# Attention scores and maxima as two 64-row tiles on a key stack without zero halves

## The chip, the cores and the metric

The kernel runs on one core of one Trainium2 chip. The metric is the device time of one execution in microseconds, lower is better. A core has TensorE (PE; its weight loads are listed apart as PEld), VectorE (DVE), ScalarE (ACT), GpSimd (POOL) and SyncE (SP), which here only issues DMAs. Each runs its own instructions in order and waits on semaphores.

## What is computed

16 batches of x, each 256 tokens by 256 features, with a condition vector of 64 numbers per batch. Four layers follow one another; all in fp32, with products of high and low parts where precision asks for it.

```
_L0: x = x + a_alpha * attention(gamma*rmsnorm(x)+beta)     # 16 heads of 16, softmax(scale*q.k)
     x = x + f_alpha * (silu(h @ gate.T) * (h @ hidden.T)) @ out.T + out_b
_L1: u = h @ up.T; val, gate = split(u); h = val * gelu(gate)
     y = quantised(h) @ ternary(down).T;  x = y + x
_L2: x = x + relu(x @ Wd_b.T + bd) @ Wu_b.T + bu            # Wd_b, Wu_b made from the condition
_L3: layer norm of x, plus tanh(condition @ lin_w.T + lin_b), scaled
```

The change touches the attention of _L0 alone: for each head the product of 256 queries and 256 keys over 16 features, its maximum over the keys, and exp(scale * (product - maximum)).

## The kernel before, in words

**The loop.** `whole` unrolls the first three and the last three runs and loops over the rest. A run works on several batches at once, each at another stage: `a` is in attention, `f` (one batch earlier) in the gated layer of _L0 and the up projection of _L1, `g` (two earlier) in the rest, `nxt` (one later) in its norm and its q, k, v projection. Every engine has its own `run` (lines 324, 411, 642, 906, 1228), written out by hand, and this order is what each engine executes. Loop periods are all alike.

**The stacks.** `project_qk` (458) puts q and k of the next batch into PSUM. ScalarE copies them as fp32r (`split_qk`, 777), VectorE subtracts (`low_qk`, 1030), so there is a high and a low part. SP writes both to HBM (`stack_qk`, 287, line 298) and reads them back as stacks (line 312), twelve loads of 128 KB: per head 16 rows of q high, q low, q high against k high, k high, k low, and row 48 for the maximum against a row of ones. Even heads lie on partitions 0 to 48, odd heads on 64 to 112. `q_stack` holds 8 pairs; `k_stack` holds 16 heads, each with the other parity's half zero (memset at line 438), so that one matmul over 128 rows gives the scores of one head. Row 48 of `q_stack` is set to zero by two small DMAs (303) while the maxima are computed, later it is filled with them (359).

**Maxima.** `max_scores(b, n)` (477) is one matmul of 512 columns: 128 queries of a pair against the 256 keys of both heads, into one of banks 0 to 2. `row_max` (1036) reduces a bank on VectorE. On TensorE's `run`, for c from 0 to 9: `gate(f, c)` (534), `max_scores(a, 2c)` and `(a, 2c+1)`, `ffn_out(f, c-2)` (550). Then `max_turn` (493) transposes the maxima, ScalarE copies them (`max_row_out`), SP puts them into row 48.

**Scores.** `scores(b, h)` (499) is two matmuls of 256 columns with the keys as weights, into bank 0 or 1; ScalarE's `exps` (798) takes a bank per head. Between them stand `mlp_down`, `norm_g`, `y_turn`, `adapter_down`, `adapter_up` of other batches and, after every four heads, `attend` (510), eight fp32 matmuls in four column tiles of 128x32, listed as 16 since each takes two passes.

**After it.** den_guess on ScalarE, `normalise` and `normalised`, `centre` and then `low_qk` of the next batch on VectorE; the write and the read of the stacks run while TensorE does `project`, `project_v` and `up` (566) and the first `gate`. `norm_a` (454, 1021) has its mean and its Newton steps in bank 4, `norm_g` (562, 1125) in bank 5.

Of the kernel before, what the change touches and what calls it, by code (L numbers as in the profile page):

```python
# [15 lines left out]
F32 = mybir.dt.float32  # L16
# [60 lines left out]
def build(nc, xT, condT, w_cond, w_qkvT, w_oT, w_ghT, w_outT, out_b, w_upT, w_downT,  # L77
          w_hyper, head_rows, adapt_w, adapt_b, bd, bu, ln_w, ln_b, lin_b, ident_in, out):
    with ExitStack() as ctx:
# [10 lines left out]


# [45 lines left out]
        k_stack = sb("k_stack", [P, H, T], F32R)  # L137
# [3 lines left out]
        zero_row = few_rows[32:32 + NPAIR, :]  # L141
# [71 lines left out]
        qk_dram_w, stack_dma = sem("qk_dram_w", 32), sem("stack_dma", 16 * 14)  # L213
# [9 lines left out]
        max_mm, max_red = sem("max_mm", 16), sem("max_red", 16)  # L223
        max_t, max_row = sem("max_t"), sem("max_row")
        s_mm, s_exp, pv_mm = sem("s_mm", 16), sem("s_exp", 16), sem("pv_mm", 4)
# [50 lines left out]
        with nc.Block() as block:  # L276

            @block.sync
            def _(sp):
# [7 lines left out]
                def stack_qk(b):  # L287
# [14 lines left out]
                    for a in range(2):  # L302
                        sp.dma_start(q_stack[64 * a + 48:64 * a + 49, :, :].bitcast(F32), zero_row).then_inc(stack_dma.sem, 16)
                    sp.wait_ge(qk_dram_w.sem, qk_dram_w.at(b))
                    for dram, dst, parts in ((q_dram, q_stack, (0, 1, 0)), (k_dram, k_stack, (0, 0, 1))):
                        for a in range(2):
                            for c, part in enumerate(parts):
                                src = dram[:, part].rearrange("(m a r) n -> a r m n", a=2, r=DH)[a]
                                at = 64 * a + DH * c
                                to = dst[at:at + DH, :, :] if dst is q_stack else \  # L310
                                    dst[at:at + DH].rearrange("r (m a) n -> r a m n", a=2)[:, a]
                                sp.dma_start(to.bitcast(F32), src).then_inc(stack_dma.sem, 16)  # L312
# [69 lines left out]
                sp.wait_ge(init_pool.sem, 2)  # L382
                sp.wait_ge(init_dve.sem, 4)
                for a in range(2):
                    sp.dma_start(k_stack[64 * a + 48:64 * a + 49].rearrange("r (m a) n -> r a m n", a=2)[:, a].bitcast(F32),
                                 one_row).then_inc(init_dma.sem, 16)
# [11 lines left out]
            def _(pool):  # L398
# [39 lines left out]
                pool.memset(k_stack[:].bitcast(F32), 0.0).then_inc(init_pool.sem, 1)  # L438
# [9 lines left out]
            def _(pe):  # L448
# [28 lines left out]
                def max_scores(b, n):  # L477
                    pair, qt = n // 2, n % 2
                    if n == 0:
                        pe.wait_ge(stack_dma.sem, stack_dma.at(b))  # L480

                    if n == 0:
                        pe.wait_ge(qk_lo.sem, qk_lo.at(b, 1))
                    if n == 1:
                        pe.wait_ge(qk_lo.sem, qk_lo.at(b, 2))
                    if n == 2:
                        pe.wait_ge(v_ready.sem, v_ready.at(b))
                    if n >= 3:
# [918 lines left out]
```

## Time and profile before

| | us |
|---|---|
| runs | 1147.42, 1151.02, 1153.07 |
| median | 1151.02 |
| profiled execution, its own span | 1152.7 |
| PE busy | 1006.3 |
| PEld busy | 848.4 |
| DVE busy | 791.2 |
| ACT busy | 534.8 |
| POOL busy | 197.4 |

The profile is one execution. PE busy adds up durations that contain the way through the array, and matmuls overlap; the distance between starts is what a matmul costs in a flow. An idle time stands in square brackets with what ended it. The last instruction that used the engine may still be listed as busy while the array stands empty, so a hole of 0.1 us between two matmuls shows in their starts alone. In the chain of waits a piece names the engine, the tile it wrote and the line; "SPq" is the issue of a DMA.

### The profile page before, as it was taken

The page shows a single profiled execution, that of the slowest core. Times are in us where ns is not written, and L with a number is a line of the kernel's source. Part 1 is how long each engine was busy: PE and PEld are TensorE (multiplying, and loading weights), DVE is VectorE, ACT ScalarE, POOL GpSimd, SP SyncE. Part 2 cuts the span into 40 slices and gives each one's busy share as a digit, 9 for nine tenths or more (in the row PEclk, how much of TensorE's full clock was granted, in tenths as well). Part 3 has the DMA queues.
Part 4 walks back from the last instruction along what each step waited for, and adds up shares of the span by engine and source line. Part 5 has one row for each costly group of instructions (what it writes and reads, how often), then busy time and mean ns, then how long its engine had stood idle before and what let it go on. Part 6 is the DMA issues. An engine that isn't in the chain of part 4 may idle for free.

```text
span 1152.7 us, 22223 instructions
## 1 busy us (share of the span) xinstructions
PE 1006.3 (87%) x7362; PEld 848.4 (74%) x7362; DVE 791.2 (69%) x1755; ACT 534.8 (46%) x1100; POOL 197.4 (17%) x235
## 2 busy tenths in 40 slices
PE   5159679999999999999999999999999999998964
PEld 4024659788887879697878878797969788886852
DVE  3445367777777777777777777877777777776552
ACT  2245264545545363645454453636364544535330
POOL 2341101111121211021111212120211112121210
PEclk9679799999999999999999999999999999999985
DMA  9998506060604224060707042241606070510000
GB/s 334 264 279 310 73 2 120 1 130 2 126 3 80 49 55 74 33 96 1 128 1 128 1 84 45 61 68 38 91 1 128 1 128 1 91 31 10 10 19 9
DMA packets 78049, 89.45 MB, mean 78 GB/s; under 512 B 18672, under 2 KB 64640, under 8 KB 75392
## 3 DMA queue, kind: packets, MB, share of 16 engines
q1 hardware_dynamic: 71792, 62.81, 28.9%
q0 software_dynamic: 2304, 16.78, 4.0%
q10 hardware_dynamic: 3920, 9.44, 2.2%
q8 instruction: 19, 0.31, 0.1%
q14 instruction: 14, 0.11, 0.0%
HBM read 63.14 MB, written 25.31 MB: 77 GB/s over the span
## 4 chain that ended last, share of the span: by engine, by line
PE 52%; DMA 17%; DVE 13%; SPq 7%; issue 5%; ACT 4%; POOL 1%; DVEq 0%; ACTq 0%; POOLq 0%
PE bank L545 14%; DMA k_stack<-k_dram 10%; PE bank L506 7%; PE bank L557 7%; PE bank L490 5%; SPq L312 5%; DMA k_dram<-probs 5%; PE bank L582 4%; PE bank L516 4%; PE bank L451 4%; DMA k_stack<-few_rows 1%; PE bank L620 1%; DVE probs L1033 1%; PE bank L593 1%; PE bank L614 1%
## 5 line engine op out<-in xcount | busy, mean ns | idle before, releaser
L1042 DVE TENSOR_REDUCE neg_max<-bank 128x2 f32<-128x512 f32 x256 | 165.2, 684 | 45.6 <-PE bank L490 45.6
L418 POOL TENSOR_TENSOR act_lo<-act_f,act_hi 128x256 fp32r<-128x256 f32 x128 | 94.4, 738 | 444.6 <-ACT act_hi L839 444.6
L804 ACT ACTIVATE probs<-bank 128x512 f32<-128x512 f32 x256 | 138.4, 592 | 37.0 <-PE bank L506 35.6
L833 ACT ACTIVATE silu_g<-bank 128x256 f32<-128x256 f32 x128 | 49.1, 384 | 219.3 <-PE bank L545 219.2
L490 PE MATMUL bank<-k_stack,q_stack 128*128 128x512 f32 x256 | 86.2, 419 | 45.2 <-DMA k_stack<-k_dram 44.3
L506 PE MATMUL bank<-q_stack,k_stack 128*128 128x256 f32 x512 | 108.3, 329 | 5.7 <-DMA q_stack<-few_rows 2.4
L506 PEld LDWEIGHTS bank<-q_stack,k_stack 128*128 128x128 f32 x512 | 76.6, 192 | 45.6 <-ACT probs L804 31.9
L582 PE MATMUL bank<-up_hi,h_hi 128*128 128x256 f32 x512 | 106.7, 289 | 1.3 <-DVE act_u L1145 0.6
L545 PE MATMUL bank<-h_hi,gh_hi 128*128 128x256 f32 x512 | 103.5, 284 | 3.6 <-DVE h_lo L1103 3.6
L545 PE MATMUL bank<-h_lo,gh_hi 128*128 128x256 f32 x512 | 103.5, 284 | 0.0
L545 PE MATMUL bank<-h_hi,gh_lo 128*128 128x256 f32 x512 | 102.9, 283 | 0.0
L582 PE MATMUL bank<-up_lo,h_hi 128*128 128x256 f32 x512 | 101.7, 280 | 0.0
L582 PE MATMUL bank<-up_hi,h_lo 128*128 128x256 f32 x512 | 101.7, 279 | 0.0
L868 ACT ACTIVATE gelu_g<-bank 128x256 f32<-128x256 f32 x128 | 49.1, 384 | 104.6 <-PE bank L582 104.0
L403 POOL TENSOR_TENSOR xc<-xc,y 128x512 f32<-128x512 f32 x16 | 20.7, 1294 | 435.5 <-DVE y L1015 435.5
L1109 DVE TENSOR_TENSOR act_f<-bank,silu_g 128x256 f32<-128x256 f32 x128 | 53.9, 421 | 56.6 <-ACT silu_g L833 55.6
L1145 DVE TENSOR_TENSOR act_u<-bank,gelu_g 128x256 f32<-128x256 f32 x128 | 54.0, 422 | 50.9 <-ACT gelu_g L868 50.9
L545 PEld LDWEIGHTS bank<-h_hi,gh_hi 128*128 128x128 f32 x512 | 81.3, 190 | 7.2 <-issue 4.5
L582 PEld LDWEIGHTS bank<-up_hi,h_hi 128*128 128x128 f32 x512 | 79.6, 189 | 5.6 <-DVE act_u L1145 4.1
L516 PE MATMUL bank<-probs,v_aug 128*32 128x256 f32 x1024 | 69.4, 389 | 14.1 <-ACT probs L804 14.1
L490 PEld LDWEIGHTS bank<-k_stack,q_stack 128*128 128x128 f32 x256 | 40.3, 193 | 53.6 <-DMA k_stack<-k_dram 35.2
L545 PEld LDWEIGHTS bank<-h_hi,gh_lo 128*128 128x128 f32 x512 | 79.5, 190 | 0.0
(150 smaller groups left out, 2193.4 us busy)
## 6 DMA issues: line engine op xcount, KB each, us to landing
hyper<-w_hyper POOLq DMA_DIRECT2D x16, 1024.0 KB, 8.2
q_stack<-q_dram SPq DMA_DIRECT2D x96, 128.0 KB
k_stack<-k_dram SPq DMA_DIRECT2D x96, 128.0 KB
q_dram<-probs SPq DMA_DIRECT2D x16, 512.0 KB, 2.8
k_dram<-probs SPq DMA_DIRECT2D x16, 512.0 KB, 3.6
delta_dram<-hyper_s ACTq DMA_DIRECT2D x16, 256.0 KB, 6.4
x_res<-xT SPq DMA_DIRECT2D x16, 256.0 KB, 7.9
out<-xc SPq DMA_DIRECT2D x16, 256.0 KB, 8.3
```

The lines of the kernel that those rows point to most:

```text
L312: sp.dma_start(to.bitcast(F32), src).then_inc(stack_dma.sem, 16)
L418: pool.tensor_tensor(act_lo[:, c % 3, :], act_f[:, c % 2, :], act_hi[:, c % 3, :].bitcast(F32), ALU.subtract).then_inc(g_lo.sem, 1)
L490: pe.matmul(bank[n % 3][:], q_stack[:, pair, qt * P:(qt + 1) * P], k_stack[:, 2 * pair:2 * pair + 2, :], start=True, stop=True).then_inc(m ...
L506: mm = pe.matmul(halves(h % 2)[:, k, :], k_stack[:, h, k * P:(k + 1) * P], q_stack[:, h // 2, :], start=True, stop=True)
L516: mm = pe.matmul(at[32 * j:32 * j + 32, t % 2, :], v_aug[:, k, 4 * t + j, :], probs[:, (4 * t + j) % SLOTS, k, :], start=(k == 0), stop=(k ...
L545: mm = pe.matmul(at[:, x, :], w[:, d, x * F + c * P:x * F + (c + 1) * P], h[:, d, :], start=(n == 0), stop=(n == 5))
L557: mm = pe.matmul(halves(3)[:, m, :], w[:, c, m * P:(m + 1) * P], h[:, c % 3, :], start=(c == 0 and m == 0 and n == 0), stop=(c == FC - 1 a ...
L582: mm = pe.matmul(at[:, x, :], h[:, d, t * P:(t + 1) * P], w[:, d, x * F + c * UW:x * F + (c + 1) * UW], start=(i == 0), stop=(i == 5))
L804: act.activation(probs[:, h % SLOTS], halves(h % 2), ACT.Exp, scale=float(H / D) ** 0.5).then_inc(s_exp.sem, 1)
L1042: dve.tensor_reduce(neg_max[:, qt, :, pair:pair + 1].rearrange("p a o -> p (a o)"), halves(n % 3), AX_X, ALU.max, negate=True).then_inc(ma ...
L1109: dve.tensor_tensor(act_f[:, c % 2, :], halves(4 + c % 2)[:, 1, :], silu_g[:, c % 2, :], ALU.mult)\
L1145: dve.tensor_tensor(act_u[:, t, c * UW:(c + 1) * UW], halves(7 - n % 2)[:, 0, :], gelu_g[:, n % 2, :], ALU.mult).then_inc(u_dve.sem, 1)
```

## The change

Scores and maxima are matmuls on 64-row tiles: `tile_position=(0, 0)` for the even heads, `(64, 0)` for the odd ones, over 48 or 49 rows, issued in turn. `k_stack` holds 8 pairs like `q_stack`, without zero halves; its memset, that of `q_stack`, the zero row and the two DMAs of line 303 are gone. `max_scores(b, d)` does two pairs for 128 queries in four matmuls of 256 columns, with one semaphore step, into two banks, one for each parity; `row_max` reduces one parity of two pairs. `scores(b, m)` does a pair of heads in four matmuls with one step; the heads rotate over banks 0, 1 and 4. So the mean and the Newton steps of `norm_a` move from bank 4 to bank 5, where `norm_g` has its own: `norm_g` waits for the third Newton step of `norm_a`, and `norm_a` stands behind `ffn_out(6)` and waits for the last `gated`. In TensorE's order `mlp_down(g, 1)` stands between the first and second pair of scores, and `norm_g` behind the second.

```diff
+        def score_bank(h):
+            return halves((0, 1, 4)[h % 3])
-        k_stack = sb("k_stack", [P, H, T], F32R)
+        k_stack = sb("k_stack", [P, NPAIR, T], F32R)
...
-                    for a in range(2):
-                        sp.dma_start(q_stack[64 * a + 48:64 * a + 49, :, :].bitcast(F32), zero_row).then_inc(stack_dma.sem, 16)
...
-                pool.memset(k_stack[:].bitcast(F32), 0.0).then_inc(init_pool.sem, 1)
...
-                    mean(bank[4][:, 0:T], h1).then_inc(n1_pe.sem, 1)
+                    mean(bank[5][:, 0:T], h1).then_inc(n1_pe.sem, 1)
...
-                def max_scores(b, n):
-                    pair, qt = n // 2, n % 2
...
-                    if n >= 3:
-                        pe.wait_ge(max_red.sem, max_red.at(b, n - 2))
-                    pe.matmul(bank[n % 3][:], q_stack[:, pair, qt * P:(qt + 1) * P],
-                              k_stack[:, 2 * pair:2 * pair + 2, :], start=True, stop=True).then_inc(max_mm.sem, 1)
+                def max_scores(b, d):
+                    m, qt = d // 2 * 2, d % 2
...
+                    if d >= 1:
+                        pe.wait_ge(max_red.sem, max_red.at(b, 2 * d - 1))
+                    for i in range(2):
+                        for a in range(2):
+                            r = slice(64 * a, 64 * a + 48)
+                            mm = pe.matmul(halves((2 * d + a) % 3)[:, i, :], q_stack[r, m + i, qt * P:(qt + 1) * P],
+                                           k_stack[r, m + i, :], start=True, stop=True, tile_position=(64 * a, 0))
+                    mm.then_inc(max_mm.sem, 1)
...
-                def scores(b, h):
...
-                    if h >= 2:
-                        pe.wait_ge(s_exp.sem, s_exp.at(b, h - 1))
+                def scores(b, m):
...
+                    if m >= 1:
+                        pe.wait_ge(s_exp.sem, s_exp.at(b, 2 * m - 1))
                     for k in range(TT):
-                        mm = pe.matmul(halves(h % 2)[:, k, :], k_stack[:, h, k * P:(k + 1) * P], q_stack[:, h // 2, :],
-                                       start=True, stop=True)
+                        for a in range(2):
+                            r = slice(64 * a, 64 * a + 49)
+                            mm = pe.matmul(score_bank(2 * m + a)[:, k, :], k_stack[r, m, k * P:(k + 1) * P], q_stack[r, m, :],
+                                           start=True, stop=True, tile_position=(64 * a, 0))
                     mm.then_inc(s_mm.sem, 1)
...
-                def norm_g(b):
+                def norm_g(b, nxt):
                     pe.wait_ge(n3_act.sem, n3_act.at(b, 1))
+                    if nxt:
+                        pe.wait_ge(n1_dve.sem, n1_dve.at(nxt, 3))
...
                         if a and c < FC:
-                            max_scores(a, 2 * c)
-                            max_scores(a, 2 * c + 1)
+                            max_scores(a, c)
...
                         if f and c >= 2:
                             ffn_out(f, c - 2)
+                        if nxt and c == FC:
+                            if starts(a):
+                                pe.wait_ge(ternary.sem, 2)
+                            if f:
+                                pe.wait_ge(g_dve.sem, g_dve.at(f))
+                            norm_a(nxt)
...
                     if a:
                         scores(a, 0)
+                    if g:
+                        mlp_down(g, 1)
+                    if a:
                         scores(a, 1)
-                    if g:
-                        mlp_down(g, 1)
                     if f:
-                        norm_g(f)
-                    if a:
-                        scores(a, 2)
-                        scores(a, 3)
+                        norm_g(f, nxt)
                     for t in range(4):
...
                             if t < 3:
-                                scores(a, 4 * t + 4)
-                                scores(a, 4 * t + 5)
+                                scores(a, 2 * t + 2)
...
                             attend(a, t)
                             if t < 3:
-                                scores(a, 4 * t + 6)
-                                scores(a, 4 * t + 7)
+                                scores(a, 2 * t + 3)
...
-                    pair, qt = n // 2, n % 2
-                    dve.wait_ge(max_mm.sem, max_mm.at(b, n + 1))
+                    d, a = n // 2, n % 2
+                    m, qt = d // 2 * 2, d % 2
+                    dve.wait_ge(max_mm.sem, max_mm.at(b, d + 1))
...
-                    dve.tensor_reduce(neg_max[:, qt, :, pair:pair + 1].rearrange("p a o -> p (a o)"), halves(n % 3), AX_X, ALU.max,
+                    dve.tensor_reduce(neg_max[:, qt, a, m:m + 2], halves(n % 3), AX_X, ALU.max,
                                       negate=True).then_inc(max_red.sem, 1)
```

## Rows read from the trace of the kernel before

**Rows 1.** Page, part 1, TensorE: busy time, share, instructions.

```profile
PE 1006.3 (87%) x7362; PEld 848.4 (74%) x7362; DVE 791.2 (69%) x1755; ACT 534.8 (46%) x1100; POOL 197.4 (17%) x235
```

**Rows 2.** Windows: stretch, length; busy us per engine (instructions), clock, DMA share, GB/s.

```profile
568.64:588.60 19.96, 19.17 (x153) 18.20 (x153) 16.22 (x33) 5.76 (x16) 5.29 (x8) 1.00 0.11 29
568.64:631.90 63.26, 59.63 (x450) 51.66 (x451) 47.66 (x108) 31.75 (x67) 10.20 (x13) 1.00 0.32 59
```

**Rows 3.** Chain of waits in one period: start us, us, what.

```profile
599.04 0.86 PE bank L614 x4
...
612.84 1.21 DVE probs L1033 x2
614.13 3.56 DMA k_dram<-probs
...
622.82 8.96 DMA k_stack<-k_dram
```

**Rows 4.** Timeline, PE: start, us, line, operation, count [idle before <- releaser].

```profile
568.64 0.72 PE L490 MATMUL bank<-k_stack,q_stack 128*128 128x512 f32 x2 [1.01 <-DMA k_stack<-k_dram]
...
588.60 0.39 PE L496 MATMUL bank<-ident,neg_max 128*16 128x128 f32 x2 [0.78 <-DVE neg_max L1042]
...
594.21 1.13 PE L451 MATMUL bank<-h,mean_w 128*128 128x256 f32 x4 [0.30 <-ACT h L757]
...
606.10 0.42 PE L516 MATMUL bank<-probs,v_aug 128*32 128x256 f32 x4 [0.94 <-ACT probs L804]
```

**Rows 5.** Timeline, PE, around the last maxima of the period.

```profile
586.25 0.40 PE L545 MATMUL bank<-h_lo,gh_hi 128*128 128x256 f32 x2
586.49 0.61 PE L490 MATMUL bank<-k_stack,q_stack 128*128 128x512 f32 x2
586.94 0.28 PE L557 MATMUL bank<-act_hi,fo_hi 128*128 128x256 f32 x1
```

**Rows 6.** Timelines, PE and PEld, short windows where scores and attend meet.

```profile
596.75 0.50 PE L506 MATMUL bank<-q_stack,k_stack 128*128 128x256 f32 x2
597.18 0.42 PE L516 MATMUL bank<-probs,v_aug 128*32 128x256 f32 x4
...
597.42 0.13 PEld L516 LDWEIGHTS bank<-probs,v_aug 128*32 128x32 f32 x4
...
597.64 0.61 PE L516 MATMUL bank<-probs,v_aug 128*32 128x256 f32 x8
598.18 0.19 PEld L506 LDWEIGHTS bank<-q_stack,k_stack 128*128 128x128 f32 x1 [0.41 <-ACT probs L804]
...
604.42 0.74 PE L506 MATMUL bank<-q_stack,k_stack 128*128 128x256 f32 x4
```

**Rows 7.** Groups by line and form, weight loads, 300 to 1000 us: busy, mean ns.

```profile
L506 PEld LDWEIGHTS bank<-q_stack,k_stack 128*128 128x128 f32 x352 | 51.8, 188 | 25.4 <-ACT probs L804 18.4 <-issue 4.1
...
L516 PEld LDWEIGHTS bank<-probs,v_aug 128*32 128x32 f32 x704 | 18.4, 109 | 24.6 <-ACT probs L804 12.6
```

**Rows 8.** Timeline of SP's DMA issues in the period.

```profile
614.55 2.02 SPq L303 DMA_DIRECT2D q_stack<-few_rows  x2
```

**Rows 9.** Timeline, ACT: exponentials 0 and 1, 2 and 3, 4 and 5, 14 and 15.

```profile
594.06 1.06 ACT L804 ACTIVATE probs<-bank 128x512 f32<-128x512 f32 x2
595.61 1.09 ACT L804 ACTIVATE probs<-bank 128x512 f32<-128x512 f32 x2 [0.48 <-PE bank L506]
...
597.41 1.07 ACT L804 ACTIVATE probs<-bank 128x512 f32<-128x512 f32 x2
...
604.96 1.08 ACT L804 ACTIVATE probs<-bank 128x512 f32<-128x512 f32 x2 [0.69 <-PE bank L506]
```

**Rows 10.** Timeline, DVE: third Newton step of norm_a.

```profile
595.76 0.42 DVE L1015 SCALAR_TENSOR_TENSOR y<-bank,y 128x256 f32<-128x256 f32 x1
```

**Rows 11.** The start: timeline of POOL, and the chain of waits.

```profile
2.03 3.53 POOL L438 MEMSET k_stack<- 128x4096 f32 x1
...
18.88 16.53 DMA k_stack<-few_rows
```

More of the change, by code:

```diff
@@ L212, in build @@
         x_in_dma, x_res_dma = sem("x_in_dma", 32), sem("x_res_dma", 32)
-        qk_dram_w, stack_dma = sem("qk_dram_w", 32), sem("stack_dma", 16 * 14)
+        qk_dram_w, stack_dma = sem("qk_dram_w", 32), sem("stack_dma", 16 * 12)
         max_dma = sem("max_dma", 32)
@@ L664, in run @@
                             max_turn(a)
-                        if nxt and c == FC:
-                            if f:
-                                pe.wait_ge(g_dve.sem, g_dve.at(f, 7))
-                            norm_a(nxt)
                         if f and c >= 2:
                             ffn_out(f, c - 2)
+                        if nxt and c == FC:
[4 more added lines that the diff above has]
+                            norm_a(nxt)
                         if starts(a) and c in (1, 3, 5, 7):
@@ L679, in run @@
                         scores(a, 0)
-                        scores(a, 1)
                     if g:
                         mlp_down(g, 1)
+                    if a:
+                        scores(a, 1)
                     if f:
-                        norm_g(f)
-                    if a:
-                        scores(a, 2)
-                        scores(a, 3)
+                        norm_g(f, nxt)
                     for t in range(4):
@@ L735, in _ @@
                     for c in range(DC):
-                        mm = pe.matmul(bank[5][:, (m * DC + c) * NB:(m * DC + c + 1) * NB],
+                        mm = pe.matmul(bank[4][:, (m * DC + c) * NB:(m * DC + c + 1) * NB],
                                        cond_w[:, m * D + c * P:m * D + (c + 1) * P], cond_t[0:C, 0:NB],
@@ L774, in guess_a @@
                         act.wait_ge(n1_dve.sem, n1_dve.at(b, back=1))
-                    guess(y1, 4, eps_rms, n1_act, b, 2)
+                    guess(y1, 5, eps_rms, n1_act, b, 2)
                 def split_qk(b):
@@ L798, in exps @@
                 def exps(b, h):
-                    act.wait_ge(s_mm.sem, s_mm.at(b, h + 1))
+                    act.wait_ge(s_mm.sem, s_mm.at(b, h // 2 + 1))
                     if h == 0:
@@ L803, in exps @@
                         act.wait_ge(pv_mm.sem, pv_mm.at(b, (h - SLOTS) // 4 + 1))
-                    act.activation(probs[:, h % SLOTS], halves(h % 2), ACT.Exp, scale=float(H / D) ** 0.5).then_inc(s_exp.sem, 1)
+                    act.activation(probs[:, h % SLOTS], score_bank(h), ACT.Exp, scale=float(H / D) ** 0.5).then_inc(s_exp.sem, 1)
                 def den_guess(b, u):
@@ L988, in _ @@
                 for c in range(DC):
-                    act.activation(tanh_t[:, c, :], bank[5][:, (14 + c) * NB:(15 + c) * NB], ACT.Tanh,
+                    act.activation(tanh_t[:, c, :], bank[4][:, (14 + c) * NB:(15 + c) * NB], ACT.Tanh,
                                    bias=lin_b_c[:, c:c + 1]).then_inc(tanh_act.sem, 1)
@@ L996, in _ @@
                 split_qk(Batch(0))
-                act.wait_ge(init_dve.sem, 4)
+                act.wait_ge(init_dve.sem, 2)
                 copy_v(Batch(0))
@@ L1293, in _ @@
                 dve.memset(eps_ln, EPS_LN).then_inc(consts.sem, 1)
-                dve.memset(q_stack[:].bitcast(F32), 0.0).then_inc(init_dve.sem, 1)
-                dve.memset(zero_row, 0.0).then_inc(init_dve.sem, 1)
                 dve.memset(one_row, 1.0).then_inc(init_dve.sem, 1)
@@ L1302, in _ @@
                 dve.wait_ge(cond_mm.sem, 1)
-                src = bank[5][:, 0:16 * NB].rearrange("p (m c b) -> p m c b", m=8, c=DC)
+                src = bank[4][:, 0:16 * NB].rearrange("p (m c b) -> p m c b", m=8, c=DC)
                 dve.wait_ge(tanh_act.sem, DC)
```

28 lines of the change are left out of this document (10 added, 18 removed).

## Prediction

> **What bounds the kernel now.** I read the page first: TensorE is busy 87% of the span [rows 1]. Then one loop period cut into stages, the chain of waits through it, and the timelines at the seams. A period lasts 63.26 us, from 568.64 to 631.90, at full clock [rows 2]. The chain through it has three kinds of stretch. In the first 18.8 us it goes from one TensorE group to the next: gate, maximum scores and ffn_out run without a gap. From 592.3 to 605.5 the scores (L506) alternate with the 16 exponentials on ScalarE; ScalarE stops for scores (0.48 us before exp 2, 0.69 before exp 14) [rows 9], TensorE for exponentials (0.94 us before the last attend) [rows 4]. Last comes a DMA stretch: low_qk, 3.56 us for the write of k, twelve issues, and 8.96 us until the stack is in SBUF [rows 3]. TensorE, busy with `up` meanwhile, waits only 1.0 us at its end [rows 4]. So a us of TensorE counts in full in the first stretch, partly in the second, and in the third only beyond that 1.0 us.
>
> **The prices.** (a) In steady flow matmuls of 256 columns start 0.12 us apart (two take 0.40, one alone 0.28) [rows 5]: the weight load of the next hides behind the one before. (b) Where the array's shape changes there is a hole. The second of two score matmuls starts at 596.75 + 0.50 - 0.28 = 596.97; the first of the 128x32 tiles starts at 597.18, 0.21 later instead of 0.12 [rows 6]. Going back, the last tile matmul starts at 597.64 + 0.61 - 0.38 = 597.87 and the next full load at 598.18, 0.31 later; a steady fp32 matmul takes 0.215 (four in L614's 0.86) [rows 3]. Either way about 0.10 us stand empty. (c) The load itself is then in the open: in the burst of four at 604.42 the last starts 0.74 - 0.28 = 0.46 after the first load, where three steady steps are 0.35 [rows 6]. A change of shape into 128-column weights thus costs 0.10 + 0.11 = 0.21 us.
> (d) Do two row tiles run at once? No row shows two of them. The nearest are the four column tiles of L516: four matmuls fit into 0.42 us of which one alone is 0.38 to 0.40, so they start within 0.03 us, and four of their loads fit into 0.13 [rows 6]. The other end is one after another. A load of 128 columns lasts 188 ns, one of 32 columns 109 [rows 7], so 128 columns hold the weight path some 128/96 x 79 = 105 ns, nearly a steady step. If the two tiles' loads had to queue, a pair would take 0.23 and nothing would be won. I take "at once", as the column tiles do.
> The Trainium skill (TensorE: Matmul & The Clock Gate, What overlaps and what doesn't) says that a load overlaps running matmuls only where its row group differs. That favours "at once"; but the loads of (a) hide behind matmuls on the same rows, so the trace does not bear out its "only".
>
> **Phase one, gate and maxima.** Removed per group: two matmuls of 512 columns, which push the next L557 from 586.49 to 586.94, 0.45 us [rows 5]. Added: four matmuls of 256 columns in two pairs between full-array work on both sides: 0.10 empty, 0.11 load, two steps of 0.115, 0.10 empty, 0.11 load, together 0.63 to 0.65. Difference +0.18. Seven of a batch's eight groups pay it; before the first TensorE stands idle for the DMA and pays nothing: 1.2 us. TensorE's 0.78 us of idle time before max_turn [rows 4] gives no cover: it waits for the last row_max, and row_max(14) now waits for the whole last group instead of half of it. VectorE has room, 16.2 of 19.96 us busy [rows 2]. **+1.2 us a batch**, 15 batches with a gate beside them: +18.
>
> **Phase two, scores and exponentials.** I stepped through it with the offsets of the rows: the second pair starts 0.22 after the group's first load (0.12 plus the open 0.11); ScalarE starts 0.32 after the last matmul's start (604.42 + 0.22, then exp 14 at 604.96); exponentials follow 0.49 apart (1.08 - 0.59); TensorE goes on 0.65 after the start of the exponential it waits for (605.45 to 606.10) [rows 4, 6, 9]. In the frame of the period shown:
> - Scores 0 wait for the maxima's DMA as before; mlp_down follows 0.1 earlier. Scores 1 now wait for exp 0 (594.06) and load at 594.71, so exp 2 starts at 595.26 instead of 595.61.
> - norm_g now waits for the third step of norm_a's Newton iteration, since both use bank 5. That step ended at 595.76 + 0.42 = 596.18 [rows 10], now at about 596.06. The mean starts at 596.12 instead of 594.21 [rows 4]. Queued behind it on TensorE are y_turn, scores 2 and attend 0; for its result wait guess_g and, behind that on ScalarE, exp 4. Exp 4 moves from 597.41 to 598.16: +0.75.
> - From there each group S of scores stands between other shapes, where it was so only next to attend. S3 loads at 599.06, S4 at 600.56, S5 at 602.00, S6 at 603.50, S7 at 604.93, each because TensorE arrives only then, not because a bank is late. Exp 6 starts at 599.60, exp 8 at 601.10, exp 12 at 604.04, exp 14 at 605.47 instead of 604.96.
> The two steps of 0.12 saved per pair of heads nearly pay for the changes of shape; the third bank for scores is rarely what is waited for. **Exp 15 ends 0.5 us later**, 16 batches: +8. All up to low_qk (den_guess, normalise, centre) hangs on it and shifts with it.
>
> **Phase three and the start.** The twelve stack loads keep size, count and order. The key stack is now contiguous in SBUF, but its source rows in HBM are cut as before: 0, and from the twelve issues and 8.96 us I see no reason for more than 0.5 either way. The two zero-row DMAs (2.02 us of SP's queue, until 616.57) [rows 8] lie within SP's wait for the write of k, which ends at 617.69 [rows 3]: their removal gains nothing. norm_a moves behind ffn_out(6), with its user guess_a still behind the table load: 0. At the start the memset of the old stack held GpSimd 3.53 us ahead of three weight loads; but the chain there runs over the ones row of the key stack, which took 16.53 us behind other loads of its queue [rows 11]: -1, within -3 and +3, since the three loads now enter a full DMA earlier.
> **Sum:** 1152.7 + 18 + 8 - 1 = 1178 on the profiled execution, whose span lies 1.7 above the median of 1151.0; on that median **1176**, with a range of its own of 1162 to 1192 (a change of shape between 0.17 and 0.25, norm_g's delay between 0.3 and 0.8).
>
> **Rivals.** *Row tiles change shape for nothing (faster).* Every row of (b) is of a column split. Then a group of maxima costs 0.23 instead of 0.45: 8 x -0.22 + 0.1 = -1.7 us, 15 times; in phase two norm_g's delay is made up and exp 15 comes 0.3 earlier, 16 times. With the start -31: 1120. It decides in phase one: below 0.11 a change, that phase gains. For it: the rows keep their weights and moving data apart without any new cut of the columns. Against: both ways, into the split and out of it, show the same 0.10.
> The Trainium skill (TensorEngine Tiling (Array Packing), Key Properties) says that a change of tiling mode, not just of tile, drains TensorE, and lists row and column splits as modes alike. By that rule this rival is out, and the L506 to L516 rows agree with it. The same page's Theoretical Speedup of up to 2x for a small dimension of 64 would, alone, give 1120.
> *Half the price.* At 0.1 a change phase one moves by 0 and phase two by 0.1 to 0.2: 1148 to 1155.
> *One after another (slower still).* A group takes 0.24 more: phase one +1.9 a batch, in phase two six groups in the chain, +1.4. +29 + 22: 1227. For it: loads of 128 columns fill the weight path, those of L516 are of 32. This is also the case in which the change doesn't do what it says.
>
> **Numbers.** Forecast 0.56, shape for nothing 0.20, half price 0.11, one after another 0.13. The range 1118 to 1194 takes in the first three and leaves out the last. 0.5% of 1151 is 5.8 us, about what a measurement of this kernel can tell from no change. Faster: the first rival and a little of the half price, 0.22. Same: 0.09. Slower: 0.69.
>
> **What would show it.** In the changed trace: the starts of the two tiles' matmuls (0.01 us apart, or 0.12); from the last gate matmul to the first load of the maxima 0.21, and again out of it; 0.64 added by a group, 0.23 or 0.87; from the stack's landing to max_turn 21.1 instead of 19.96; exp 4 0.75 and exp 15 0.5 later against square_g; TensorE's wait for the stack still near 1 us; a period near 65.0. I am wrong if changes of shape are free for rows, if VectorE's maxima set phase one instead of TensorE, if TensorE's 1.0 us behind the DMA turns into a longer or shorter wait, or if the start moves by more than 3 us.

## The result and the profile after

| | before | after |
|---|---|---|
| median, us | 1150.06 (1147.42 to 1153.07, 4 runs) | 1187.87 (1183.63 to 1189.88, 4 runs) |
| ratio, 95% interval | | 1.0333 [1.0303, 1.0362] |
| profiled execution, span | 1152.7 | 1185.2 |
| mean granted clock | 0.959 | 0.941 |

The changed kernel is slower by 37.8 us. The forecast was slower by 25.

Page of the changed kernel, part 1. It answers to [rows 1].

```profile
PE 1015.9 (86%) x7618; PEld 821.1 (69%) x7618; DVE 793.9 (67%) x1753; ACT 537.6 (45%) x1100; POOL 193.8 (16%) x234
```

TensorE did 256 matmuls more and was busy 10 us longer, the span grew by 32.5. So 23 us of the loss stand outside TensorE's busy time.

Windows of the changed kernel: from the landing of the stack to max_turn, and one whole period. The columns are those of [rows 2].

```profile
584.32:605.31 20.99, 20.23 (x168) 17.97 (x168) 16.43 (x33) 6.32 (x18) 5.21 (x8) 1.00 0.11 27
584.32:649.78 65.46, 59.36 (x468) 49.36 (x468) 48.40 (x108) 32.45 (x69) 10.18 (x13) 1.00 0.32 57
```

The first stretch takes 20.99 where [rows 2] have 19.96, with VectorE no busier.

PE's timeline of the changed kernel around a group of maxima, then its weight loads, then max_turn.

```profile
588.56 0.40 PE L545 MATMUL bank<-h_lo,gh_hi 128*128 128x256 f32 x2
588.89 0.50 PE L486 MATMUL bank<-k_stack,q_stack 48*128 48x256 f32 x4
589.32 0.38 PE L557 MATMUL bank<-act_hi,fo_hi 128*128 128x256 f32 x1
589.54 0.28 PE L557 MATMUL bank<-act_hi,fo_lo 128*128 128x256 f32 x1
...
588.89 0.30 PEld L486 LDWEIGHTS bank<-k_stack,q_stack 48*128 48x128 f32 x4
...
605.36 0.39 PE L493 MATMUL bank<-ident,neg_max 128*16 128x128 f32 x2 [0.81 <-DVE neg_max L1042]
```

Read it by starts, as [rows 5]. The last gate matmul starts at 588.56 + 0.40 - 0.28 = 588.68. The first load of the maxima comes 0.21 later and the first full load after them at 589.32. The four tile matmuls fill 0.50, so the second pair starts 0.22 after the first (0.12 plus 0.10 of open load); the records' own starts put the two tiles of a pair 0.004 and 0.002 us apart. From the last gate matmul to ffn_out it is 0.64; in [rows 5] it is 586.94 - 586.37 = 0.57, and there the next matmul follows after the steady 0.12, here after 0.22. That makes 0.17 a group here, where gate matmuls stand before it and ffn_out behind it.

PE's, ACT's and DVE's timelines of the changed kernel where norm_g now waits. They answer to [rows 4, 9, 10].

```profile
611.49 0.50 PE L506 MATMUL bank<-q_stack,k_stack 49*128 49x256 f32 x4 [0.93 <-ACT probs L803]
612.88 1.13 PE L446 MATMUL bank<-h,mean_w 128*128 128x256 f32 x4 [0.89 <-DVE y L1014]
...
610.85 2.26 ACT L803 ACTIVATE probs<-bank 128x512 f32<-128x512 f32 x4
614.04 0.48 ACT L760 ACTIVATE y<-bank,columns 128x256 f32<-128x256 f32 x1 [0.93 <-PE bank L446]
...
614.92 1.09 ACT L803 ACTIVATE probs<-bank 128x512 f32<-128x512 f32 x2
...
612.40 0.42 DVE L1014 SCALAR_TENSOR_TENSOR y<-bank,y 128x256 f32<-128x256 f32 x1
```

The third Newton step of norm_a ends at 612.82, norm_g's mean starts at 612.88, guess_g (L760) at 614.04 and exp 4 at 614.92: 4.07 us after exp 0, where before it is 597.41 - 594.06 = 3.35 [rows 9]. Scores 1, the only matmuls between 610.56 (the end of mlp_down) and 612.88, stand between two holes of about 0.9 us.

The same place 195 us earlier, in one of the three middle periods (of 13) in which something more happens. Timeline of PE, then windows; the granted clock is the number after the five engines:

```profile
416.16 0.50 PE L506 MATMUL bank<-q_stack,k_stack 49*128 49x256 f32 x4 [0.94 <-ACT probs L803]
417.54 2.07 PE L446 MATMUL bank<-h,mean_w 128*128 128x256 f32 x4 [0.88 <-DVE y L1014]
419.40 1.06 PE L609 MATMUL bank<-ident,mlp_y 128*128 128x128 f32 x4
...
414.00:417.30 3.30, 1.71 (x16) 1.02 (x14) 2.65 (x8) 2.20 (x5) 0.00 (x0) 1.00 0.00 0
417.30:420.70 3.40, 3.17 (x10) 2.36 (x12) 1.71 (x5) 1.39 (x4) 0.00 (x0) 0.50 0.00 0
420.70:424.00 3.30, 3.30 (x36) 1.92 (x38) 3.16 (x8) 2.17 (x5) 0.00 (x0) 1.00 0.00 0
```

The granted clock is at half, 1.2 instead of 2.4 GHz, just when norm_g can start: four matmuls take 2.07 instead of 1.13. Before it fell TensorE had stood in the two holes, busy 1.71 of 3.30 us. The forecast has no term for this.

**Where the 32.5 us between the two profiled executions are.** Each batch cut at its first maximum scores:

| stretch | us |
|---|---|
| up to batch 1 (129.33 against 127.44) | +1.9 |
| batch 1 to batch 2 (66.05 against 62.91) | +3.1 |
| 13 middle periods, maxima: 1.09 each | +14.2 |
| the same, exp 0 to exp 4 without the falls: 0.70 each | +9.1 |
| the same, exp 4 to exp 15: -0.26 each | -3.4 |
| the same, before exp 0 and behind exp 15: 0.11 each | +1.4 |
| the same, falls of the clock, 3 periods | +7.0 |
| the same, DMA stretch | -2.2 |
| behind the last first maxima (143.5 against 142.1) | +1.4 |

### The profile page after: what moved, and what is told of

Same layout as the page of the kernel before. It is cut to its first block, busy times and chain, and to the rows that moved or that the text cites. A ratio compares the mean times of both kernels' runs of the same rounds, so it can differ in the third digit from the quotient of the medians.

```text
span 1185.2 us, 22613 instructions
## 1 busy us (share of the span) xinstructions
PE 1015.9 (86%) x7618; PEld 821.1 (69%) x7618; DVE 793.9 (67%) x1753; ACT 537.6 (45%) x1100; POOL 193.8 (16%) x234
## 3 DMA queue, kind: packets, MB, share of 16 engines
q1 hardware_dynamic: 71280, 62.54, 27.8%
## 4 chain that ended last, share of the span: by engine, by line
PE 51%; DMA 19%; DVE 13%; SPq 7%; issue 5%; ACT 5%; POOL 0%; DVEq 0%; ACTq 0%; POOLq 0%
PE bank L545 14%; DMA k_stack<-k_dram 11%; PE bank L557 6%; SPq L310 6%; PE bank L486 5%; DMA k_dram<-probs 5%; PE bank L506 4%; PE bank L516 4%; PE bank L584 3%; PE bank L446 3%; DMA q_stack<-few_rows 3%; PE bank L622 2%; PE bank L602 2%; PE bank L616 2%; DVE probs L1032 1%
## 5 line engine op out<-in xcount | busy, mean ns | idle before, releaser
L545 PE MATMUL bank<-h_hi,gh_hi 128*128 128x256 f32 x512 | 107.4, 291 | 3.6 <-DVE h_lo L1103 3.6
L486 PE MATMUL bank<-k_stack,q_stack 48*128 48x256 f32 x512 | 67.2, 342 | 42.1 <-DMA k_stack<-k_dram 38.5
L506 PEld LDWEIGHTS bank<-q_stack,k_stack 49*128 49x128 f32 x512 | 39.9, 193 | 69.6 <-ACT probs L803 54.7
L516 PE MATMUL bank<-probs,v_aug 128*32 128x256 f32 x1024 | 72.0, 401 | 17.9 <-ACT probs L803 17.9
L557 PE MATMUL bank<-act_hi,fo_hi 128*128 128x256 f32 x256 | 85.7, 335 | 0.9 <-POOL act_lo L414 0.9
L506 PE MATMUL bank<-q_stack,k_stack 49*128 49x256 f32 x512 | 66.8, 341 | 22.8 <-ACT probs L803 17.1
L486 PEld LDWEIGHTS bank<-k_stack,q_stack 48*128 48x128 f32 x512 | 40.2, 194 | 64.8 <-DMA k_stack<-k_dram 31.9
```

What stands on the lines that cost most here:

```text
L486: mm = pe.matmul(halves((2 * d + a) % 3)[:, i, :], q_stack[r, m + i, qt * P:(qt + 1) * P], k_stack[r, m + i, :], start=True, stop=True, ti ...
L506: mm = pe.matmul(score_bank(2 * m + a)[:, k, :], k_stack[r, m, k * P:(k + 1) * P], q_stack[r, m, :], start=True, stop=True, tile_position= ...
L516: mm = pe.matmul(at[32 * j:32 * j + 32, t % 2, :], v_aug[:, k, 4 * t + j, :], probs[:, (4 * t + j) % SLOTS, k, :], start=(k == 0), stop=(k ...
L545: mm = pe.matmul(at[:, x, :], w[:, d, x * F + c * P:x * F + (c + 1) * P], h[:, d, :], start=(n == 0), stop=(n == 5))
L557: mm = pe.matmul(halves(3)[:, m, :], w[:, c, m * P:(m + 1) * P], h[:, c % 3, :], start=(c == 0 and m == 0 and n == 0), stop=(c == FC - 1 a ...
```

## The experiments

The table gives medians over twelve middle periods, so single falls of the clock don't enter, except in scores_alone, where nearly every period has one. "Falls" counts stretches at half clock in the 13 middle periods; all but two begin around norm_g's mean, 1.2 to 3.3 us after exp 0, where the mean starts 2.0 after it. The two others, in after_again at 201.7 us and in tile_by_tile at 197.6, follow a wait for the stack of 1.6 and 1.8 us. Times are medians. The kernel before took 1150.06 beside after, 1148.06 beside maxima_alone to early_newton, 1149.37 beside scores_early to tile_by_tile and 1150.67 beside the last three.

| kernel | stack to last row_max | exp 0 to 4 | exp 4 to 15 | period | falls | time | ratio [95%] |
|---|---|---|---|---|---|---|---|
| before | 19.91 | 3.36 | 8.04 | 63.18 | 0 | 1150.06 | |
| after | 20.99 | 4.06 | 7.78 | 64.70 | 3 | 1187.87 | 1.0333 [1.0303, 1.0362] |
| maxima_alone | 20.99 | 3.35 | 8.04 | 63.92 | 0 | 1170.48 | 1.0219 [1.0158, 1.0280] |
| maxima_full_array | 20.21 | 3.36 | 8.04 | 63.25 | 0 | 1160.19 | 1.0110 [1.0058, 1.0161] |
| scores_alone | 19.90 | 5.55 | 7.80 | 64.48 | 12 | 1175.85 | 1.0235 [1.0172, 1.0298] |
| early_newton | 20.98 | 3.11 | 7.78 | 63.39 | 0 | 1166.19 | 1.0163 [1.0114, 1.0211] |
| scores_early | 19.92 | 3.11 | 7.78 | 62.35 | 0 | 1143.44 | 0.9940 [0.9907, 0.9973] |
| scores_filled | 19.92 | 4.14 | 7.78 | 63.49 | 0 | 1157.00 | 1.0078 [1.0046, 1.0109] |
| tile_by_tile | 21.04 | 4.21 | 7.80 | 65.75 | 6 | 1190.13 | 1.0360 [1.0323, 1.0397] |
| start_memset | 21.00 | 4.07 | 7.78 | 65.19 | 4 | 1197.97 | 1.0398 [1.0329, 1.0467] |
| after_again | 20.98 | 4.55 | 7.78 | 65.55 | 9 | 1206.11 | one run |
| before_again | 19.90 | 3.36 | 8.03 | 62.45 | 0 | 1150.16 | one run |

### The maxima alone

The kernel before with row tiles for the maxima, on its old stack:

```diff
+                    for i in range(2):
+                        for a in range(2):
+                            r = slice(64 * a, 64 * a + 48)
+                            mm = pe.matmul(halves((2 * d + a) % 3)[:, i, :], q_stack[r, m + i, qt * P:(qt + 1) * P],
+                                           k_stack[r, 2 * (m + i) + a, :], start=True, stop=True, tile_position=(64 * a, 0))
```

> The kernel before with one part of the change: the maxima as 64-row tiles, on the old key stack; scores, banks and start as before. Theory (a change of array shape costs 0.10 us of empty array and 0.11 us of open weight load each way, the pair of tiles runs at once): the stretch from the stack's landing to the last row_max grows from 19.90 to 20.98 us in 15 batches, +16; the first batch, without a gate beside its maxima, may add up to 4 more if its clock stays at half there: 1166 to 1171. Rival (the 13 us that the changed kernel is above the forecast come from this part too, over something that grows with the batches): 1175 or more. Rival (the loss is in the stack's layout or its loads): 1150, no change.

Measured: +22.4 us, the first stretch 20.99, phase two as before. 1170.48 lies in the range of the theory.

And the same program with the same four matmuls over all 128 rows, so that only the shape is taken away:

```diff
-                            mm = pe.matmul(halves((2 * d + a) % 3)[:, i, :], q_stack[r, m + i, qt * P:(qt + 1) * P],
-                                           k_stack[r, 2 * (m + i) + a, :], start=True, stop=True, tile_position=(64 * a, 0))
+                            mm = pe.matmul(halves((2 * d + a) % 3)[:, i, :], q_stack[:, m + i, qt * P:(qt + 1) * P],
+                                           k_stack[:, 2 * (m + i) + a, :], start=True, stop=True)
```

> The same program as maxima_alone, with the same four matmuls of 256 columns in the same order, into the same banks, with the same waits, but each over the whole array instead of a 64-row tile. Theory: without a change of shape a group costs 4 x 0.117 = 0.47 us instead of 0.66, so the stretch stays at 19.9 to 20.1 and the time at 1150 to 1154. Rival (the loss comes from four matmuls in the place of two, or from VectorE waiting for the whole group): 1160 or more.

Measured: +12.1 us and 1160.19. My 1150 to 1154 was too low; it is the rival's case, 1160 or more. PE's timeline of maxima_full_array, the last group of a period and max_turn, then the same of the changed kernel:

```profile
591.30 0.40 PE L546 MATMUL bank<-h_lo,gh_hi 128*128 128x256 f32 x2
591.54 0.64 PE L490 MATMUL bank<-k_stack,q_stack 128*128 128x256 f32 x4
592.02 0.29 PE L558 MATMUL bank<-act_hi,fo_hi 128*128 128x256 f32 x1
...
593.89 0.39 PE L497 MATMUL bank<-ident,neg_max 128*16 128x128 f32 x2 [1.01 <-DVE neg_max L1043]
...
603.14 0.50 PE L486 MATMUL bank<-k_stack,q_stack 48*128 48x256 f32 x4
```

Four full-array matmuls cost the flow 0.48 (591.54 to 592.02), the two of 512 columns 0.45 [rows 5]. But the first stretch is 0.30 longer, 0.23 of it idle time before max_turn (1.01 against 0.78 [rows 4]): row_max can start only when the whole group is done. By subtraction, 0.78 of the +1.08 a batch belongs to the shape and 0.30 to one semaphore step for four matmuls.

The two don't simply add up, though. From the start of the last group to max_turn it is 2.11 before (586.49 to 588.60 [rows 4, 5]), 2.35 in maxima_full_array, but 2.22 in the changed kernel (603.14 to 605.36): two tiles at once finish the group earlier, and TensorE's idle time before max_turn is 0.81, nearly the 0.78 of before. So in the changed kernel only 0.11 of the loss stands behind the start of the last group. The other 0.97 arises on the way to it. In the median of the middle batches the last group starts 17.86 us after the first before the change, 17.92 in maxima_full_array and 18.83 in the changed kernel. From group to group four of the seven steps grow by 0.17 to 0.19, the three behind the first, second and seventh group by 0.07 to 0.10.

The step costs more in the first batch, which has no gate beside it and where TensorE waits for VectorE between groups. PE's timeline of the changed kernel, start of batch 0:

```profile
59.50 0.80 PE L486 MATMUL bank<-k_stack,q_stack 48*128 48x256 f32 x4 [22.05 <-DMA k_stack<-k_dram]
61.17 0.80 PE L486 MATMUL bank<-k_stack,q_stack 48*128 48x256 f32 x4 [0.88 <-DVE neg_max L1042]
```

Every other group of the first batch waits for row_max. The batch's maxima take 12.5 us before, 15.3 in maxima_full_array and 16.3 in maxima_alone and after. The forecast had counted this batch at zero. Windows over these maxima, before, maxima_full_array, after:

```profile
63.82:76.35 12.53, 11.32 (x48) 3.80 (x48) 9.95 (x16) 5.27 (x5) 3.13 (x2) 0.84 0.99 353
63.70:79.00 15.30, 11.75 (x64) 6.00 (x64) 10.29 (x16) 5.88 (x6) 4.17 (x2) 0.81 0.90 339
59.50:75.82 16.32, 13.08 (x64) 4.84 (x64) 10.31 (x16) 5.62 (x5) 5.29 (x3) 0.50 0.83 309
```

The first two have nearly the same granted clock, so 2.8 us are the price of the grouping; the programs that keep the old maxima lie between 12.5 and 13.2 here, which makes it 2.1 to 2.8. The last 1.0 can be the shape or the clock, which in maxima_alone and after is at half all through: no run separates them.

### The scores alone, and the wait of norm_g

The kernel before with the scores in row tiles, three banks for them, norm_a in bank 5 and norm_g's wait; maxima, stack and start as before.

```diff
+                        for a in range(2):
+                            r = slice(64 * a, 64 * a + 49)
+                            mm = pe.matmul(score_bank(2 * m + a)[:, k, :], k_stack[r, 2 * m + a, k * P:(k + 1) * P], q_stack[r, m, :],
+                                           start=True, stop=True, tile_position=(64 * a, 0))
...
+                    if nxt:
+                        pe.wait_ge(n1_dve.sem, n1_dve.at(nxt, 3))
```

> The kernel before with the other part alone: the scores as 64-row tiles over banks 0, 1 and 4, norm_a in bank 5 and norm_g behind its Newton steps; old key stack, old maxima, old start. Theory (norm_g's wait holds exp 4 back by 0.7 us, the rest of the scores gives 0.26 back): +0.44 a batch, 16 batches, +7; where the hole ahead of norm_g lets the clock fall to half, 1.5 to 4 us more each time, three times in the changed kernel's trace: 1157 to 1166. Rival (norm_g's wait is absorbed): 1146 to 1151.

Measured: +27.8 and 1175.85, above the 1157 to 1166 of my theory. In 12 of 13 middle periods the clock falls at norm_g. PE's timeline and windows of scores_alone:

```profile
671.29 0.50 PE L512 MATMUL bank<-q_stack,k_stack 49*128 49x256 f32 x4 [0.85 <-ACT probs L810]
672.77 2.07 PE L454 MATMUL bank<-h,mean_w 128*128 128x256 f32 x4 [0.97 <-DVE y L1021]
...
672.30:675.70 3.40, 2.93 (x10) 2.14 (x10) 1.84 (x4) 1.42 (x4) 0.00 (x0) 0.51 0.00 0
```

To take the wait away without a race, I moved what it waits for. In the changed kernel VectorE does norm_a's Newton steps ahead of `scaled_y`, not behind it:

```diff
+                    if nxt:
+                        newton_a(nxt)
                     if g:
                         scaled_y(g)
```

> The changed kernel with one step moved: on VectorE the three Newton steps of norm_a stand ahead of scaled_y, so that bank 5 is free 1.3 us earlier. Theory (that wait delays exp 4 by 0.7 us in every batch and opens the hole in which the clock falls in some): exp 0 to exp 4 goes from 4.06 to about 3.4 us, -10; no half clock in the middle batches, -7 on the profiled execution: 1170 to 1178. Rival (the clock falls for the row tiles' own sake, since they fill less of the array): the half-clock stretches stay, 1177 or more. Rival (VectorE pays as much for the new order as TensorE wins): 1188.

Measured: 1166.19, below my 1170 to 1178 and 21.7 below the changed kernel. In ratios to before it is 1.0163 against 1.0333, some 20 us. exp 0 to exp 4 went from 4.06 to 3.11, where I had expected 3.4: 16 x 0.95 = 15.2 us. And no middle period falls to half clock (7.0 in the profiled execution of after). Batch 1, ahead of the middle periods, still has a stretch of 20.5 us at half clock, and lasts 69.5 us. PE's timeline of early_newton:

```profile
610.01 0.51 PE L506 MATMUL bank<-q_stack,k_stack 49*128 49x256 f32 x4 [0.94 <-ACT probs L803]
610.45 1.13 PE L446 MATMUL bank<-h,mean_w 128*128 128x256 f32 x4
```

The mean follows the scores at once; only the hole ahead of scores 1 is left. With the same move on scores_alone, the maxima stay as they were:

> scores_alone with the Newton steps of norm_a ahead of scaled_y, as in early_newton: full-array maxima, old stack, scores as row tiles. Theory (the score tiles themselves gain, and what they lost was lost by norm_g's wait): exp 0 to exp 4 takes 3.11 us and exp 4 to exp 15 7.78, as in early_newton, instead of 3.36 and 8.04 before; the maxima's stretch stays at 19.90; -0.5 a batch, 16 batches, -8: 1138 to 1144 where the kernel before has 1148 to 1150. Rival (the DMA stretch takes back what is won, since TensorE then arrives earlier at the same landing): 1146 to 1150.

Measured over 12 runs against 22: 1143.44, ratio 0.9940, that is 3.1 to 10.7 us faster than the kernel before, or less than one per cent. It beats both kernels. By stages: -0.25 to exp 4, -0.26 to exp 15, 16 times, -8. This is what the scores' part of the change is worth once nothing hangs on bank 5. It holds the row tiles, the third bank, one semaphore step per pair and the new places of mlp_down and norm_g. No run has the same order and banks with full-array scores, so the share of the row tiles is not shown.

### Is it the hole or the row tiles that lets the clock fall?

scores_alone with seven further matmuls ahead of norm_g's wait. They multiply gate weights with themselves into a free half bank that nobody reads; they change nothing but what the array does meanwhile.

```diff
+                        for _ in range(7):
+                            pe.matmul(halves(3)[:, 0, :], gh_hi[:, 0, 0:P], gh_hi[:, 0, 0:T], start=True, stop=True)
                         pe.wait_ge(n1_dve.sem, n1_dve.at(nxt, 3))
```

> scores_alone with seven more full-array matmuls, whose result nobody reads, in the hole ahead of norm_g: behind its wait for the squares, ahead of its wait for the Newton steps. They take 0.9 us of idle time and change no wait. Theory (the clock falls to half because the array is idle in that hole): the half-clock stretches in the middle batches are gone, exp 0 to exp 4 takes about 4.1 us as in the one undisturbed period of scores_alone, instead of 5.55: -1.4 a batch, about 1158. Rival (the row tiles themselves let the clock fall, by filling fewer rows): the half-clock stretches stay and the time is 1176 or more.

Measured: 1157.00, 18.9 below scores_alone. PE's timeline and windows of scores_filled:

```profile
657.60 0.51 PE L512 MATMUL bank<-q_stack,k_stack 49*128 49x256 f32 x4 [0.85 <-ACT probs L812]
658.03 1.10 PE L572 MATMUL bank<-gh_hi 128*128 128x256 f32 x7
659.07 1.13 PE L454 MATMUL bank<-h,mean_w 128*128 128x256 f32 x4
...
657.60:661.00 3.40, 3.40 (x23) 2.66 (x23) 3.00 (x8) 2.25 (x5) 0.00 (x0) 1.00 0.00 0
```

norm_g waits as long as in scores_alone, but the clock stays at full, in all 13 periods. exp 0 to exp 4 is 4.14 instead of 5.55, and 13 x 1.4 is 18 us. Work that nobody needs made this kernel faster. By itself this run leaves a second reading: the seven matmuls fill the whole array, so they could also make up for what the row tiles leave empty. scores_early answers it. It has the same row tiles and the first of the two holes (0.85), only not the one at norm_g, and no middle period falls. So the row tiles alone don't let the clock fall; it takes the hole at norm_g. Whether the same two holes around full-array scores would do it too, no run shows. And 4.14 - 3.11 = 1.03 a period is the bare price of the wait.

### Does the order of the four matmuls matter?

The prediction left open whether the two tiles run at once because they are issued in turn. The changed kernel with both matmuls of the upper tile first, then both of the lower:

```diff
-                    for i in range(2):
-                        for a in range(2):
+                    for a in range(2):
+                        for i in range(2):
```

> The changed kernel with the order of the four matmuls of each group turned: both of tile 0 first, then both of tile 64. Nothing else. Theory (the two tiles run at once only when they are issued in turn, since matmuls start in order): a group takes one step of 0.115 us more, phase one +0.9 a batch, phase two +0.5 to +0.7: +20 to +25 on the changed kernel, 1208 to 1213. Rival (TensorE reorders, or the tiles' concurrency is worth little here): 1188, no change.

Measured: 1190.13, the rival's number. The ratio to before is 1.0360 against 1.0333, and the two intervals overlap. PE's and PEld's timelines of tile_by_tile:

```profile
589.20 0.51 PE L486 MATMUL bank<-k_stack,q_stack 48*128 48x256 f32 x4 [0.90 <-DMA k_stack<-k_dram]
...
589.19 0.31 PEld L486 LDWEIGHTS bank<-k_stack,q_stack 48*128 48x128 f32 x4 [1.10 <-issue]
```

The group is 0.01 longer than in order by turns. The records start in pairs again: 589.198 and 589.205, then 589.415 and 589.428. So here the expectation failed: that two tiles run at once does not depend on issue in turn. The records don't name the tile. That each pair is an upper beside a lower one, though both uppers were issued first, is inferred from this: two matmuls on the same rows start 0.12 apart everywhere else. That the new order reached the engine at all shows in the small distances: in the median of the middle groups of maxima the two of a pair start 0.007 and 0.008 apart, where it is 0.003 in the changed kernel, and the group lasts 0.508 instead of 0.502.

### The start, and both kernels once more

After the first seven runs it was open whether the falls and the start were chance. So both kernels once more, and the changed one with GpSimd's clears put back ahead of its first loads:

```diff
+                pool.memset(pad[:], 0.0).then_inc(init_pool.sem, 1)
+                pool.wait_ge(init_pool.sem, 2)
+                pool.memset(pad[:], 0.0).then_inc(init_pool.sem, 1)
```

> The changed kernel once more, unchanged, for a second execution with rows. Open is where some 13 us above the forecast came from. Theory A: the fall of the clock in the hole ahead of the mean of norm_g is a matter of chance in every execution, and the second one shows it again in some of the middle periods, perhaps in others than at 417, 806 and 1004 us; each costs 1.5 to 6 us. Theory B: it was a disturbance of that one execution, and the second has no middle stretch at half clock and lies near 1178. For the start: the first maximum scores came at 59.5 us in the changed kernel and at 63.8 in the kernel before; if that is the change, it is 59.5 again, and if it varies from execution to execution, it lies anywhere from 59 to 65, and the first two periods (69.8 and 66.1 us) come out otherwise too. I take theory A, and the start as varying: 1184 to 1190 in time.

> The kernel before once more, unchanged, for a second execution with rows: where its first maximum scores lie (63.82 us in the first profile) and whether its middle periods again hold no stretch at half clock. If the start varies from execution to execution, they lie anywhere from 59 to 65 here; if it belongs to the kernel, within 0.5 of 63.8. I expect it to vary, no middle stretch at half clock, and 1147 to 1153 in time.

> The changed kernel with the old work of GpSimd put back at the start: two clears of a pad of 2048 columns ahead of its first weight loads, in length like the clears of the old stacks. If the removed memset is worth the 4 us by which the first maxima come earlier in the changed kernel (59.5 against 63.8 us), they go back to 63 to 64 and the time rises to 1190 to 1192. If the start is set by the ones row of the key stack behind other loads, as the prediction had it, the time stays at 1186 to 1190 (minus one to plus one against the changed kernel) and the first maxima lie wherever this execution puts them, 59 to 65. I expect the second.

The changed kernel showed nine middle stretches at half clock and took 1206.11, far above my 1184 to 1190; the kernel before none and 1150.16. start_memset took 1192.6 to 1201.0, above my 1186 to 1190, with four stretches in its profile; beside a changed kernel of 1206.11 that says nothing against the clears. So the falls belong to the changed kernel, their number varies from execution to execution, and with it the time. How long one can last, by a window of after_again:

```profile
423.60:433.80 10.20, 9.53 (x48) 5.72 (x52) 5.69 (x13) 4.53 (x10) 0.00 (x0) 0.50 0.00 0
```

A short fall costs 1.5 us (5.55 against 4.06 to exp 4), a long one 4.3 (5.70 + 10.43 against 11.84 from exp 0 to exp 15). The four long ones in all profiles are those that begin earliest, 1.25 to 1.34 us after exp 0; the short ones at norm_g begin 1.45 to 3.30 after it. Why is open.

At the start I was wrong on both sides. The first maxima come at 59.33 with the clears and at 59.50 and 60.35 without, so the memset sets nothing; but it does not vary freely either. All six profiles with row tiles in the maxima have them at 59.3 to 61.1; the kernel before (twice) and the four others have them at 62.2 to 65.4. The chains of waits of after_again, before_again, maxima_alone and maxima_full_array, in this order, from 30 us on:

```profile
34.61 7.56 DMA k_dram<-probs
...
33.62 17.26 DMA k_dram<-probs
...
32.78 7.49 DMA k_dram<-probs
...
33.91 16.75 DMA k_dram<-probs
```

The first write of k takes 6.2 to 7.6 us in the six profiles with row-tile maxima and 14.1 to 17.4 in the six without, though maxima_alone and maxima_full_array differ only in the lines of the maxima, which run later. Why is open. It brings nothing: by batch 1 the former lie at 129.3 to 131.5 and the latter at 124.7 to 130.7.

## Why the prediction was right, and where its sum fell short

- **The price of a change of shape, 0.21 and 0.10 of it empty.** Held: 0.21 from the last gate matmul to the first tile load, 0.21 from the last pair's start (589.11) to the next full load, instead of 0.12 each, and 0.10 of open load each way, at full clock. Row tiles pay what column tiles pay. "Shape for nothing" and "half price" are out. The Trainium skill (TensorEngine Tiling (Array Packing), Key Properties), by which a change of mode drains the engine, agrees with these rows.
- **Two row tiles at once.** Held, 0.002 to 0.004 us apart; "one after another" is out. Counted as in the prediction, a group takes 0.62 (from 588.80, when the next full matmul was due, to 589.42, 0.12 ahead of 589.54); forecast were 0.63 to 0.65.
- **Phase one, +1.2 a batch.** 1.08, in maxima_alone and after alike, but the sum hit by two errors that nearly cancel. Seven groups at 0.18 would be 1.26 by the start of the last group; measured are 0.97, since next to the first group and to the bf16 transposes a group adds only 0.07 to 0.10. And the last row_max, which waits for its whole group, was named but given no price; behind the last group 0.11 are lost, in maxima_full_array without the tiles 0.25.
- **Batch 0 at nothing.** Wrong, +3.8 in that batch's maxima, 2.1 to 2.8 of it from the grouping, the rest from the shape or the half clock. TensorE "stands idle" there, but it does so in turn with VectorE, each waiting for the other, and a coarser semaphore step lengthens such a loop.
- **Phase two.** Exp 4 was to come 0.75 later and comes 0.70 later; the rest was to win back 0.25 and wins 0.26. The sum of 0.5 a batch came out as 0.44, and 0.11 more around it.
- **The clock.** This term is missing, and nothing in the range stood for it: the range was made of the price of a change and norm_g's delay. That 1187.87 still lies below its 1192 is luck. In after_again, at 1206.11, the same kernel lies outside. The prediction's own walk had scores 1 at 594.71 and the mean at 596.12, so the hole was on paper, and it took the 1.00 of [rows 2] as given for the new kernel. Summed over the middle periods the falls cost 7 us in the profiled execution and some 19 in after_again, with nine stretches at half clock. In batch 1 the clock is at half again from 168.1 to 174.9, while den_guess to low_qk last 1.8 longer (9.74 against 7.92): most of the +3.1.
- **The start, -1 within 3.** The first maxima came 4.3 earlier, outside the 3 that the prediction allowed; batch 1 came 1.9 later. That the memset counts for nothing held.
- **The DMA stretch, 0.** TensorE waited 6.1 us for the stack between 300 and 1000 us, 8.7 before: within what was allowed. This stretch also varies by itself: before and before_again, the same program, differ by 0.73 in the period (63.18 and 62.45) while the other stages agree within 0.03.

By the stages without falls, 16 batches at about 1.6 are some 26, near the forecast's 25; the other 12 us of the 37.8 are the clock and the first two batches.

Still open: why the same hole halves the clock in 12 of 13 periods in scores_alone and in 3 to 9 in the changed kernel (it was not tried to move the hole in time), and why the first write of k is short with row-tile maxima.

## What to carry over

A dense second operand that lets two small tiles run at once pays only where it replaces more steps than its two seams cost: here a group saved two steps of 0.12 and paid 0.2 at each seam. In the maxima that was a loss; in phase two the whole of the change came out ahead, with the share of the tiles not shown. When a bank is freed by putting two users into another, list what waits for the slower of the two and move that work ahead of it first: here this one move was worth some 20 us. And ask of every new hole in TensorE's stream not only how long it is but what the clock does behind it.

## What the hardware showed that was not expected

Two holes of 0.9 us around 0.5 us of matmuls were followed by a granted clock of 0.5, 1.2 instead of 2.4 GHz, in up to 12 of 13 periods, and seven unread matmuls, 1.04 us in one of the holes, kept the clock up in all of them (scores_alone, scores_filled). The Trainium skill (TensorE: Matmul & The Clock Gate, A second HAM failure mode: psum-queue depth-cycling) tells of a bf16 kernel that cycles through its PSUM banks, in which short idle times between groups let the clock swing between its two levels. These runs agree, for the matmuls of this kernel, and put 1.5 to 4.3 us on one fall.

Matmuls of two row tiles issued as upper, upper, lower, lower start in pairs 0.007 and 0.013 us apart (tile_by_tile). The Trainium skill (TensorE: Matmul & The Clock Gate, The mechanism) has matmuls start and end strictly in order. By that rule the second upper one would have held back the lower ones by at least 0.12, and the starts would come as one, two, one instead of two and two. The trace does not agree, as far as pairs tell: the records don't name the tile.
